# Shared layers of a routed feed-forward computed turned, the first experts' row lists spread over more steps, and the second attention's values and keys projected sooner

## The reference, cut to what matters

```python
# block 0
x = x + cross_attention(layernorm(x), ctx, bias)         # 16 heads, 77 keys
flat = layernorm(x)                                      # 2048 x 256
scores = softmax(flat @ router_w.T + router_bias)        # 32 experts
topk_scores, topk_idx = top_k(scores, 4)                 # normalised to sum 1
h = silu(flat @ gate_w[e].T) * (flat @ up_w[e].T)        # 128 wide, each expert e
out = sum(topk_scores * (h @ down_w[e].T))               # over the 4 chosen
out = out + (silu(flat @ sgate_w.T) * (flat @ sup_w.T)) @ sdown_w.T   # shared, 512 wide
x = x + out
# block 1
x = x + cross_attention(layernorm(x), ctx, mask)         # biases on q, k, v, o
x = x + relu(layernorm(x) @ w1[e] + b1[e]) @ w2[e] + b2[e]   # 8 experts, 1024 wide, top 1
```

## Time and profile before

| | |
|---|---|
| median of 3 runs | 761.55 us (760.32 to 763.07) |
| the profiled execution: its time, its span | 761.38 us, 759.5 us |
| busy share of the span: PE, PEld, DVE, ACT, POOL | 94%, 77%, 59%, 48%, 36% |
| chain that ended last, by engine | PE 69%, DVE 19%, issue 5%, ACT 4% |
| mean DMA rate over the span | 136 GB/s |

### The profile page before, as it was taken

How to read it: one execution, slowest core, us unless ns; L and a number is a source line. 1 busy time by engine, 2 the same in 40 slices (tenths; PEclk the granted TensorE clock), 3 DMA queues, 4 the chain that set the end, 5 groups by cost and what they waited for, 6 DMA issues and landing times.

```text
span 759.5 us, 15888 instructions
## 1 busy us (share of the span) xinstructions
PE 713.4 (94%) x4674; PEld 586.3 (77%) x4675; DVE 447.8 (59%) x1662; ACT 368.2 (48%) x1240; POOL 277.0 (36%) x335
## 2 busy tenths in 40 slices
PE   8999999899998999999999899998988999999994
PEld 5788888656666888888866588777865999999993
DVE  4799999449946433433445799999973222223321
ACT  2899999422222555554552788887831121221220
POOL 1022111000033555555507677771103343434421
PEclk9899999999999999999999999999998999999998
DMA  7543334320034555555963247774511656455540
GB/s 178 199 146 110 128 105 153 120 68 22 7 104 79 162 162 161 164 160 159 132 124 94 67 129 208 222 213 139 155 56 47 217 182 202 152 202 188 173 132 6
DMA packets 64328, 103.08 MB, mean 136 GB/s; under 512 B 20161, under 2 KB 42129, under 8 KB 64004
## 3 DMA queue, kind: packets, MB, share of 16 engines
q1 hardware_dynamic: 52996, 74.19, 31.2%
q0 software_dynamic: 10976, 27.22, 14.3%
q10 hardware_dynamic: 288, 0.79, 0.3%
HBM read 82.83 MB, written 22.07 MB: 138 GB/s over the span
## 4 chain that ended last, share of the span: by engine, by line
PE 69%; DVE 19%; issue 5%; ACT 4%; DMA 1%; POOL 0%; DVEq 0%; another core or an unknown queue 0%; ACTq 0%; SPq 0%; POOLq 0%
PE bank L1502 11%; PE bank L1517 10%; PE bank L1448 8%; PE bank L991 7%; PE bank L1461 4%; PE bank L897 3%; PE bank L966 3%; PE bank L1331 2%; PE bank L975 2%; PE bank L937 2%; PE bank L1439 2%; DVE X L1625 2%; DVE U L1816 2%; DVE R L2051 2%; DVE mx L1634 1%
## 5 line engine op out<-in xcount | busy, mean ns | idle before, releaser
L720 ACT ACTIVATE U<-U,mx 128x77 f32<-128x77 f32 x512 | 134.6, 350 | 17.0 <-issue 8.2
L651 POOL DMA_INDIRECT U<-normed,idx_all x95 | 90.4, 952 | 140.4 <-PE bank L1439 71.4
L1448 PE MATMUL bank<-R,U 128*128 x380 | 98.2, 381 | 0.0
L1502 PE MATMUL bank<-X,R 128*128 128x128 f32 x736 | 85.9, 275 | 0.0
L1502 PEld LDWEIGHTS bank<-X,R 128*128 128x128 f32 x736 | 84.1, 192 | 0.1
L1517 PE MATMUL bank<-R,X 128*128 (+1 forms) x368 | 83.1, 379 | 0.0
L2185 DVE TENSOR_TENSOR U<-U,bank 128x128 f32<-128x128 f32 x95 | 27.3, 287 | 84.3 <-issue 77.3
L1517 PEld LDWEIGHTS bank<-R,X 128*128 128x128 f32 x368 | 68.2, 190 | 8.4
L604 POOL DMA_INDIRECT R<-expert_out,slot x64 | 62.2, 972 | 33.0 <-DMA expert_out<-xr 16.9
L1448 PEld LDWEIGHTS bank<-R,U 128*128 128x128 f32 x380 | 64.8, 190 | 5.3
L2213 DVE TENSOR_SCALAR X<-bank,U 128x128 f32<-128x128 f32 x92 | 25.9, 344 | 64.6 <-PE bank L1502 47.3
(11 more groups left out here) (262 smaller groups left out, 1510.6 us busy)
## 6 DMA issues: line engine op xcount, KB each, us to landing
R<-in_w SPq DMA_DIRECT2D x21, 1024.0 KB
R<-in_w SPq DMA_DIRECT2D x40, 256.0 KB
R<-in_gu SPq DMA_DIRECT2D x8, 1024.0 KB, 5.4
expert_out<-U SPq DMA_DIRECT2D x48, 128.0 KB
expert_out<-xr SPq DMA_DIRECT2D x47, 128.0 KB
normed<-xr SPq DMA_DIRECT2D x32, 128.0 KB
R<-in_down SPq DMA_DIRECT2D x8, 512.0 KB, 3.7
x<-X SPq DMA_DIRECT2D x16, 128.0 KB
```

The source lines that it names most:

```text
L651: pool.indirect_dma_start(xg0[i % NXG], None, xn_d[0], bass.IndirectOffsetOnAxis(idx_all[:, i:i + 1], 0)).then_inc(EX[0]["gath"][i % NXG], 16)
L720: ins = act.activation(sc[u][:, h * S2:(h + 1) * S2], sc[u][:, h * S2:(h + 1) * S2], ACT.Exp, bias=mx[u][:, h:h + 1])
L1448: mm = pe.matmul(bank[2 + u][:, 0:2 * F0], xgT0[u][:, c, :], gu_w[:, c, bass.ds(e, 1), :].rearrange("p a n -> p (a n)"), start=(c == 0), s ...
L1502: mm = pe.matmul(bank[1 + 2 * v + f // 4][:, (f % 4) * P:(f % 4 + 1) * P], w1_of[v][:, c, f * P:(f + 1) * P], xgT1[v][:, c, :], start=(c = ...
```

## The change

Three edits and one number:

1. The shared layer is computed turned. Weights and rows change places in the gate and up matmuls: 128 columns of the weights are held and the turned rows of the tile are streamed. One half is now 4 x 2 matmuls of 128 columns instead of 2 of 512. The product of SiLU and up comes out with the hidden dimension on the partitions, as the down product needs it, so the four transposes, ScalarE's copy and `hsT` fall away, for tiles 12 to 15 too. The VectorE product now waits until the down product that read its buffer has run.
2. The lists take two tiles a step over eight steps (t = 3 to 10) instead of three a step over six. Tiles 13 and 14 are in step t = 10, the last tile 15 at that step's end, behind the down product; `rows0` follows at t = 10 instead of t = 8.
3. `kv_v_mm(1)` moves from t = 10 to t = 8 and no longer waits for `idx_all`; `kv_k_mm(1)` moves from t = 11 to t = 9; both write `bank[5]`. `values_of_ctx1` moves to VectorE's t = 8. `keys(1)` stays at t = 11, and `sp` still waits for `idx_all` before the mask, the late rows and `kv_values(1)`.
4. `keep_busy(23)` at the start becomes `keep_busy(17)`.

```diff
-            keep_busy(23)
+            keep_busy(17)
...
-                    for c in range(KC):
-                        mm = pe.matmul(bank[2 * v + a][:, :], xT[:, c, :], sgu_w[:, c, a * FS:(a + 1) * FS],
-                                       start=(c == 0), stop=(c == KC - 1))
+                    for f in range(FS // P):
+                        for c in range(KC):
+                            mm = pe.matmul(bank[2 * v + a][:, f * P:(f + 1) * P],
+                                           sgu_w[:, c, a * FS + f * P:a * FS + (f + 1) * P], xT[:, c, :],
+                                           start=(c == 0), stop=(c == KC - 1))
...
-                if t == ND - 2:
-                    pe.wait_ge(R0["idx_all"], 1)
+                if t == ND - 4:
                     kv_v_mm(1)
-                if t == ND - 1:
+                if t == ND - 3:
                     kv_k_mm(1)
-                if has(t, lo, hi):
-                    pe.wait_ge(SH["h"], t + 1)
-                    need(pe, SH["ht"], t)
-                    for c in range(FS // P):
-                        mm = pe.transpose(bank[5][:, c * P:(c + 1) * P], hs[u][:, c * P:(c + 1) * P], ident[:, :])
-                    mm.then_inc(SH["ht_mm"], 1)
...
-                if 4 <= t < 9:
-                    for a in range(3 * t - 11, 3 * t - 8):
+                if 4 <= t < 11:
+                    for a in range(2 * t - 7, 2 * t - 5):
                         rows_of_tiles(a)
...
+                if t == 10:
+                    rows_of_tiles(NT - 1)
...
+                    need(dve, SH["dn_mm"], t)
...
-                    if 3 <= t < 8:
-                        tiles_of(3 * t - 8)
-                    if t == 8:
-                        rows0()
+                    if 3 <= t < 11:
+                        tiles_of(2 * t - 5)
                 shared(t, lo, hi)
                 if lo == 0:
                     if t == 2:
                         tiles_of(0)
-                    if 3 <= t < 8:
-                        tiles_of(3 * t - 7)
-                        tiles_of(3 * t - 6)
-                    if t == ND - 2:
+                    if 3 <= t < 10:
+                        tiles_of(2 * t - 4)
+                    if t == 10:
+                        rows0()
+                    if t == ND - 4:
                         values_of_ctx1()
```

More of the change, by code:

```diff
@@ L190, in build @@
         o = temp_at
-        hs[0], o = cut(U, o, (FS,))
-        hs[1], o = cut(U, o, (FS,))
+        hs[0], o = cut(U, o, (FS // P, P))
+        hs[1], o = cut(U, o, (FS // P, P))
         th, o = cut(U, o, (FS,))
-        hsT, o = cut(U, o, (FS // P, P))
         assert o <= TEMP_END
@@ L274, in build @@
         hsd = [None, None]
-        hsd[0], o = cut(R2, o, (FS,))
-        hsd[1], o = cut(R2, o, (FS,))
+        hsd[0], o = cut(R2, o, (FS // P, P))
+        hsd[1], o = cut(R2, o, (FS // P, P))
         thd, o = cut(R2, o, (FS,))
-        hsTd, o = cut(R2, o, (FS // P, P))
         rows_d = []
@@ L314, in build @@
                   for t in range(NT)]
-        kv_v = [[bank[2 + b][0:S2, 0:D] for b in range(B)], [bank[7][0:S2, b * D:(b + 1) * D] for b in range(B)]]
-        kv_k = [[bank[m][:, 0:B * S2] for m in range(KC)], [bank[7][:, m * B * S2:(m + 1) * B * S2] for m in range(KC)]]
+        kv_v = [[bank[2 + b][0:S2, 0:D] for b in range(B)], [bank[5][0:S2, b * D:(b + 1) * D] for b in range(B)]]
+        kv_k = [[bank[m][:, 0:B * S2] for m in range(KC)], [bank[5][:, m * B * S2:(m + 1) * B * S2] for m in range(KC)]]
         phase_end = sem("phase_end")
@@ L766, in step @@
                         exps(t, n, 0)
-                        late_turned(NT - 1)
                     if on(t, 1):
@@ L1374, in shared @@
                 if has(t, lo, hi):
-                    pe.wait_ge(SH["ht"], t + 1)
+                    pe.wait_ge(SH["h"], t + 1)
                     need(pe, SH["x"], t)
                     for c in range(FS // P):
-                        mm = pe.matmul(bank[6][:, 0:D], hsT[:, c, :], sdown_w[:, c, :], start=(c == 0),
+                        mm = pe.matmul(bank[6][:, 0:D], hs[u][:, c, :], sdown_w[:, c, :], start=(c == 0),
                                        stop=(c == FS // P - 1))
                     mm.then_inc(SH["dn_mm"], 1)
+                if t == 10:
+                    rows_of_tiles(NT - 1)
             def late_rows(a):
@@ L1390, in late_half @@
             def late_half(a, g):
-                for c in range(KC):
-                    mm = pe.matmul(bank[2 * (a % 2) + g][:, :], xrT[:, c, :], sgu_w[:, c, g * FS:(g + 1) * FS],
-                                   start=(c == 0), stop=(c == KC - 1))
+                for f in range(FS // P):
+                    for c in range(KC):
+                        mm = pe.matmul(bank[2 * (a % 2) + g][:, f * P:(f + 1) * P],
+                                       sgu_w[:, c, g * FS + f * P:g * FS + (f + 1) * P], xrT[:, c, :],
+                                       start=(c == 0), stop=(c == KC - 1))
                 mm.then_inc(SH["gu_mm"][g], 1)
@@ L1405, in late_up, with late_down @@
                 late_half(a, 1)
-            def late_turned(a):
+            def late_down(a):
                 pe.wait_ge(SH["h"], a + 1)
[L1410 to L1417, removed]
                 pe.wait_ge(SH["x"], a)
                 for c in range(FS // P):
-                    mm = pe.matmul(bank[6][:, 0:D], hsTd[:, c, :], sdown_w[:, c, :], start=(c == 0),
+                    mm = pe.matmul(bank[6][:, 0:D], hsd[a % 2][:, c, :], sdown_w[:, c, :], start=(c == 0),
                                    stop=(c == FS // P - 1))
@@ L2128, in shared_hidden @@
                     dve.wait_ge(SH["gu_mm"][1], t + 2)
-                    dve.tensor_tensor(hs[u], th, bank[2 * u + 1][:, :], ALU.mult).then_inc(SH["h"], 1)
+                    need(dve, SH["dn_mm"], t)
+                    dve.tensor_tensor(hs[u].rearrange("p c n -> p (c n)"), th, bank[2 * u + 1][:, :],
+                                      ALU.mult).then_inc(SH["h"], 1)
             def late_hidden(a):
@@ L2134, in late_hidden @@
                 dve.wait_ge(SH["gu_mm"][1], a + 1)
-                dve.tensor_tensor(hsd[a % 2], thd, bank[2 * (a % 2) + 1][:, :], ALU.mult).then_inc(SH["h"], 1)
+                dve.wait_ge(SH["dn_mm"], a - 1)
+                dve.tensor_tensor(hsd[a % 2].rearrange("p c n -> p (c n)"), thd, bank[2 * (a % 2) + 1][:, :],
+                                  ALU.mult).then_inc(SH["h"], 1)
             def late_sum(a):
```

15 lines of the change are left out of this document (removed).

## The result

| kernel | median us | executions | ratio to before, 95% interval |
|---|---|---|---|
| before | 763.26 | 7 | |
| after | 767.81 (762.56 to 770.96) | 7 | 1.0064 [1.0032, 1.0095] |

The change made the kernel slower by 0.6%, above the predicted range of 755.5 to 762.0 us. The profiled execution took 762.56 us, the shortest of the seven. Its mean granted clock was 0.984; the four above 767 us had 0.971 to 0.973. The one trace is thus the mild case.

The account below looks back on a forecast made before the run. TensorE's own queue and its standstills were taken to bound the kernel. Start -1.3, shared stage 0.0, clock and round trip +0.8, tiles 12 to 15 -2.2 sum to -2.7: 761.38 to 758.7 us, range 755.5 to 762.0.

Parts of the forecast that it names:

- The start: Kernel start: six fewer filling matmuls end 1.33 us sooner and the gain is passed on; -1.3 us, bounds 0 and -1.3.
- The turned layer: Shared layer: a tile pays 0.13 us, saves the 0.44 turning, loads hidden; 0.86 less before the first list tile.
- The -2.9: First list tile to second gathered tile: the turned layer saves 2.9 us by nine turnings and 16 halves.
- The keys: Keys' projection in the shared stage: TensorE waits 1.8 us for VectorE's values, 0.5 longer than the old wait.
- The new wait: Before the first gathered tile's transposes: TensorE stands still for the whole gather; 4.0 us from `idx_all`, bounds 2.4 and 5.4.
- The clock: At the first gather: TensorE idle 4.6 us; a fall, held about even, doubles the down product, +1.7 us.
- the +0.8: On top of the shared stage: clock fall and values' round trip together, +0.8 us, from 0 to +2.5.
- The values' round trip: Behind `idx_all` in SyncE's queue: late by 1 to 4 us, up to 3 covered; late values hold up VectorE and TensorE.
- The slower rival: Values' round trip so late that it alone decides; stall from 2.7 + 0.8 us eats all gains; chance 0.06.
- Tiles 12 to 15: Second attention: turning and copy gone, -1.25 us sure, up to -2.4 more upstream; taken as -2.2.
- The first experts: Stage of the first experts: same instructions before and after, costed at nothing apart from the first tiles.
- the stage up to the second gathered tile: Shared stage: turned layer's savings go into the two waits; even at 0.0 us, from -1.6 to +1.4.

Follow-up runs that it names:

- turned_only: Kernel before with only the shared layer computed turned; lists, values and keys, and 23 filling matmuls as before: ratio 0.9966 to before.
- mask_after: Changed kernel, but SyncE issues the mask, late rows and values' round trip only once the first gathered tile has landed: ratio 1.0103 to before.
- fill23: Changed kernel with 23 filling matmuls at the start instead of 17: ratio 1.0052 to before.
- fill_gather: Changed kernel with 27 filling matmuls (5.9 us) ahead of the first gathered tile's transposes: ratio 1.0141 to before.
- changed_again: The changed kernel run once more, unaltered, on chip B: ratio 1.0056 to before.
- old_kv: Changed kernel with the values' projection back at t = 10 and the keys' at t = 11: ratio 0.9958 to before.
- late_index: Changed kernel with three list tiles a step over six steps as before, but `idx_all` still written only at t = 10: ratio 1.0028 to before.

## Why the prediction was wrong, step by step

- **The start** held: -1.3 forecast; the values' projection began at 7.61 to 8.76 us in four traces with 23 filling matmuls (mean 8.3) and at 6.55 to 7.45 in the others with 17 (mean 7.1), and the first attention took 131.2 us either way where its clock stayed full. The gain is carried.
- **The turned layer** held in TensorE's own work: -0.86 forecast before the first list tile, -0.73 measured; loads stay under the matmuls, 3.73 us for x32. The -2.9 from there on was not measured by itself: turned_only shows -2.01 there, with 1.8 us more of waiting for list tiles. The steps of the changed kernel came 6.18 us apart instead of 6.34: the forecast added 0.82 for 8 list matmuls, the busy time of the earlier trace rows, which overlaps the next row; on the chain they take 0.66.
- **The keys** held as to the wait: 1.8 forecast, 2.04 measured. The step failed in what follows the wait: it names no clock there, and the up product behind it took 1.5 us longer. The prediction asked about the clock only for 4.6 us of idling; of seven traces with this wait of 2.04, six show the clock falling behind it.
- **The new wait** is the step that failed most. "I take 4.0", with an upper bound of 5.4 from the earlier trace rows, was too low: it was 6.1. The rows of the bound are from a stretch with a DMA share of 0.15 (576 to 580 us before). Here the share was 0.96, because the same `idx_all` releases SyncE's mask and rows. The prediction knew these 1.1 MB, but let only the values suffer from them. The Trainium skill, "DMA: Bandwidth & Descriptors", section "Anatomy of one DMA — SWDGE (gpsimd) path", gives about 2.0 us fixed plus the bytes, by which 2.3 can be estimated for these 128 KB. mask_after's 3.2 from issue to use is 0.9 above that, with GpSimd's instruction of 1.08 us in it; after's 4.75 is 2.4 above.
- **The clock** at the gather fell and cost 1.5 to 1.8 us in the down product alone; the +0.8, which was for it and the round trip together, was half its price. Row 572 of the earlier trace rows had spoken for the fall. The Trainium skill, "TensorE: Matmul & The Clock Gate", Part 1, has idle TensorE at half rate; all nine traces with a wait of 4 us or more for the first gather agree.
- **The values' round trip** didn't stop VectorE in the changed kernel; no row of it waits for `v_rows` there. The slower rival named it as the danger: it is real, but only when SyncE's queue is held back (mask_after).
- **Tiles 12 to 15**, "-1.25 is sure, up to -2.4": -1.9 measured on chip C. With the late view nothing is left of it: the second attention took 173.1, 170.2 and 170.3 us in the first trace and on chips B and D (the first with 3.4 us of the lower clock) against 170.28 in the trace of before. The late view of TensorE's results was in no rival.
- **The first experts**, "I cost them at nothing": 0.4 to 0.5 us longer in both pairs of traces.

In sum: the stage up to the second gathered tile was put at 0.0 + 0.8 and cost +5.4. Counted from the first list tile, that is 2.1 more of waiting for the gather (6.1 for 4.0), 1.3 more behind it (4.2 us from the transposes to the second gathered tile for 2.1, less the 0.8), 1.6 for the clock behind the keys, 0.2 for their wait and 0.3 for the last list tile, less 1.0 for the shorter steps: 4.5, for a gap of 4.6. With the rest it makes the +2.2 of the traces on chip C. The range of the stage, -1.6 to +1.4 and up to +2.5 on top, did not hold these errors, because all the large ones were on the same side.

Why the whole measured 1.0064, 1.0056 and 0.9985 on three chips is explained only in part. The late view, which C doesn't have, could be 1.9 to 3.0 of the 5.4 us between B and C; but chip A doesn't have it either, and fill23 measured 1.0052 there.

What stays open: what makes TensorE's results be seen late on some chips (at full size it goes with the turned late tiles, but that is all the runs show), why the changed kernel is no slower than before on chip C, and why fill_gather loses 10 us behind the place that it mends. The spread between executions of one kernel, 758 to 771 us for the changed one, comes with the clock. A line through the 12 executions of changed_again gives 0.7 us for each us lost to the clock (one less the mean granted clock, times the span). Where the clock falls outside the waits (0 to 13.7 us of the lower clock before the shared stage, whatever the kernel) was not settled.

## What to carry over

Three of the four edits are good together: the turned layer, the sooner values and keys and the shorter filling, with the old lists, give 0.987 to 0.990. With the fourth the kernel measured 1.006, 1.006 and 0.999, so it lost most or all of it, and the sooner projections turned from a gain into a loss beside it (old_kv, 0.996). The main part is shown by late_index: the fourth edit spread VectorE's work at the price of the distance between an index list and the first use of its gather. Ask of a spread-out step what its last piece releases and how much work then stands between; and price a gather with the DMA load that the same event starts, not by one that ran alone.

A wait on TensorE may have to be counted with the next product at half clock: the wait of 2.04 us cost 3.5 with the up product behind it, that of 6.65 us 8.2 with the down product. After the first gather's wait the clock was down in every trace; behind the 2 us of the keys in six of seven, so there it is a chance and not a certainty.

## What the hardware showed

- The gather of one tile, issue to use: 3.2 us at a DMA share of 0.17, 4.75 at 0.96.
- Behind an idle time of 2.04 us the granted clock fell to its half level (0.66 over 210 to 215 us), though TensorE was busy right up to it and after it; the same wait in fill23 (2.03 us) left it at full. In or just behind waits of 4.1 to 6.75 us for the first gather it fell in all nine traces.
- VectorE and ScalarE saw results of turned late tiles about 2 us and more after the matmuls were listed as done, both at the same moment, on chips B and D and in the first trace, and not on A and C.
